# Attention layer on one core: query, key and value weights split in SBUF and turned by DMA instead of TensorE

## The reference, cut to what matters

```python
xn = layernorm(x)                                   # 2048 x 512
q  = (xn @ wq).reshape(b, s, 16, 192)               # per head 128 "nope" + 64 "rope" columns
kva = xn @ wkv_a                                    # 128 latent + 64 rope columns
ckv = rmsnorm(kva[..., :128]) * kv_norm_scale
kv = (ckv @ wkv_b).reshape(b, s, 16, 256)           # per head k_nope (128), v (128)
scores = (q_nope @ k_nope^T + rope(q_pe) @ rope(k_pe)^T) * 192 ** -0.5, causal
out = softmax(scores) @ v, heads side by side @ wo
x + out + (xn @ sum_r factors[r]) / sqrt(8) + bias
```

## Time and profile before

| | us |
|---|---|
| median of 3 runs | 1497.58 |
| profiled execution, first to last instruction (its span) | 1496.9 |
| PE busy | 1469.3 (98% of the span) |
| DVE busy | 1014.5 (68%) |
| ACT busy | 965.7 (65%) |
| POOL busy | 911.3 (61%) |
| DMA queue of SP | 74.2% of 16 engines |

### The profile page before, as it was taken

How to read it: one execution, slowest core, us unless ns; L and a number is a source line. 1 busy time by engine, 2 the same in 40 slices (tenths; PEclk the granted TensorE clock), 3 DMA queues, 4 the chain that set the end, 5 groups by cost and what they waited for, 6 DMA issues and landing times.

```text
span 1496.9 us, 25751 instructions
## 1 busy us (share of the span) xinstructions
PE 1469.3 (98%) x7908; PEld 755.5 (50%) x7908; DVE 1014.5 (68%) x2563; ACT 965.7 (65%) x2404; POOL 911.3 (61%) x919
## 2 busy tenths in 40 slices
PE   6999999999999999999999999999999999999998
PEld 5544555555555545445444444445545555555554
DVE  7877677877777766656556565556666666676777
ACT  7877767677876567566566666665546665654554
POOL 3688777776665456575465656566645655664553
PEclk9999999999999999999999999999999999999999
DMA  6599999988777597787577677886856677754564
GB/s 202 152 199 203 211 193 186 191 163 158 157 157 132 127 193 149 140 178 139 118 145 141 137 133 145 173 151 130 162 112 136 137 139 152 156 141 95 115 132 110
DMA packets 646615, 227.84 MB, mean 152 GB/s; under 512 B 599376, under 2 KB 612176, under 8 KB 646096
## 3 DMA queue, kind: packets, MB, share of 16 engines
q1 hardware_dynamic: 646480, 226.20, 74.2%
HBM read 65.67 MB, written 17.83 MB: 56 GB/s over the span
## 4 chain that ended last, share of the span: by engine, by line
PE 92%; POOL 2%; DVE 2%; ACT 2%; DMA 1%; issue 1%; SPq 0%; POOLq 0%; DVEq 0%; ACTq 0%
PE ps L426 18%; PE ps L428 18%; PE ps L427 18%; PE ps L577 7%; PE ps L582 7%; PE ps L583 7%; PE ps L578 7%; PE ps L579 7%; POOL st L1408 2%; ACT ex L812 1%; DMA acc<-x_in 0%; DVE stats L944 0%; PE ps L450 0%; DVE acc L1227 0%; DMA pT<-st 0%
## 5 line engine op out<-in xcount | busy, mean ns | idle before, releaser
L1408 POOL TENSOR_TENSOR st<-ex,st 128x512 f16<-128x512 f32 (+3 forms) x640 | 637.8, 1015 | 488.9 <-ACT st L822 478.8
L812 ACT ACTIVATE ex<-ps,nm,scales 128x512 f32<-128x512 f32 (+3 forms) x640 | 452.0, 709 | 456.3 <-DVE nm L1193 439.8
L1174 DVE TENSOR_REDUCE gm<-ps 128x1 f32<-128x512 f32 (+1 forms) x384 | 249.0, 669 | 170.0 <-PE ps L583 166.0
L822 ACT ACTIVATE st<-ex 128x512 f16<-128x512 f32 (+3 forms) x640 | 343.0, 562 | 6.1 <-ACT ex L812 0.4
L577 PE MATMUL ps<-kTh,q 128*128 128x512 f16 (+3 forms) x640 | 222.3, 347 | 4.5 <-ACT ex L812 2.1
L426 PE MATMUL ps<-pT,vH 128*128 128x512 f16 (+3 forms) x640 | 222.1, 347 | 2.9 <-DMA pT<-st 2.9
L582 PE MATMUL ps<-kRh,q 128*128 128x512 f16 (+3 forms) x640 | 222.2, 347 | 0.0
L583 PE MATMUL ps<-kRl,q 128*128 128x512 f16 (+3 forms) x640 | 222.1, 347 | 0.0
L579 PE MATMUL ps<-kTh,q 128*128 128x512 f16 (+3 forms) x640 | 222.1, 347 | 0.0
L578 PE MATMUL ps<-kTl,q 128*128 128x512 f16 (+3 forms) x640 | 222.1, 347 | 0.0
L427 PE MATMUL ps<-pT,vH 128*128 128x512 f16 (+3 forms) x640 | 222.1, 347 | 0.0
(11 more groups left out here) (202 smaller groups left out, 2144.3 us busy)
## 6 DMA issues: line engine op xcount, KB each, us to landing
wA<-w_abs SPq DMA_DIRECT2D x48, 256.0 KB, 2.9
wV<-w_vo SPq DMA_DIRECT2D x48, 256.0 KB, 2.9
pT<-st SPq DMA_TRANSPOSE x640, 3.2
fland<-factors_in SPq DMA_DIRECT2D x28, 256.0 KB, 3.1
wP<-w_pe SPq DMA_DIRECT2D x24, 256.0 KB, 3.0
wsq<-wq_in SPq DMA_DIRECT2D x16, 256.0 KB, 3.8
wso<-wo_in SPq DMA_DIRECT2D x16, 256.0 KB, 3.0
w_abs<-wA SPq DMA_DIRECT2D x16, 256.0 KB, 2.2
```

The lines of the kernel that those rows point to most:

```text
L812: e.activation(ex[:, n % NEX, 0:keys], s_bank(n)[:, 0:keys], ACT.Exp, bias=nm[:, (i * QT + r) % 4:(i * QT + r) % 4 + 1], scale=scales[:, p ...
L822: e.activation(stage(n, keys)[:, :, 0, :], ex[:, n % NEX, 0:keys].rearrange("p (t n) -> p t n", n=P), ACT.Copy).then_inc(z["a_pH"], 1)
L1174: e.tensor_reduce(m, b, AX_X, ALU.max).then_inc(z["v_max"], 1)
L1408: e.tensor_tensor(s[:, :, 1, :], ex[:, n % NEX, 0:keys].rearrange("p (t n) -> p t n", n=P), s[:, :, 0, :], ALU.subtract).then_inc(z["g_pL" ...
```

## The change

The split now comes before the turn. ScalarE reads fp32 weights in SBUF and writes the high parts into new tiles wtq and wtk (`wq_high`, `kv_high`), VectorE writes the low parts beside them (`wq_low`, `kv_low`), and SyncE issues one DMA_TRANSPOSE for the query part (`turn_wq`, 8 blocks of 128x128 fp16) and one for the key and value parts (`turn_kv`, 4 blocks; 2 where only one of them is due). TensorE's transposes and the PSUM banks that they took are gone; `w_abs` and `w_vo` wait for the DMAs. From unit 1 on, "wabs" moves from row 2 to the start of row 3; "wvo" stays in row 2. The high parts are in ScalarE's list at the end of row 0 (unit 0: row 1), the low parts in VectorE's at row 1 (unit 0: row 2), the turns in SyncE's list behind the row-1 transposes (unit 0: behind those of row 2).

```diff
@@ fills @@
-        out += [[("tq", 1), ("tkv", 1), ("sq1", 2)], [("wabs", 1), ("nrm", 2), ("wpe", 2)],
+        out += [[("sq1", 2)], [("wabs", 1), ("nrm", 2), ("wpe", 2), ("tq_hi", 2), ("tkv_hi", 2)],
                 [("tq", 2), ("tkv", 2), ("q", 1), ("wpe_low", 2)], [("wabs", 2)]][r]
...
+    if r == 3 and i and i + 2 < H:
+        out.insert(0, ("wabs", i + 2))
     if r == 0:
-        if i % 2 and i + 2 < H:
-            out.append(("tq", i + 2))
+        if i and i + 2 < H:
+            out.append(("tq_hi", i + 2))
+        if i and i + 2 <= H + 2:
+            out.append(("tkv_hi", i + 2))
...
     if r == 1:
         if i and i % 2 == 0 and i + 2 < H:
-            out += [("wpe", i + 2), ("tq", i + 2)]
+            out.append(("wpe", i + 2))
+        if i and i + 2 < H:
+            out.append(("tq", i + 2))
         if i and i + 2 <= H + 2:
             out.append(("tkv", i + 2))
...
     if r == 2:
         if 1 <= i <= H:
             out.append(("wvo", i - 1))
-        if i and i + 2 < H:
-            out.append(("wabs", i + 2))
@@ TensorE @@
             def w_abs(h):
-                e.wait_ge(z["v_tq"], h + 1)
-                e.wait_ge(z["v_tkv"], h + 1)
+                e.wait_ge(z["d_tq"], 16 * (h + 1))
+                e.wait_ge(z["d_tkv"], 16 * (h + 1))
...
             def w_vo(h):
                 e.wait_ge(z["v_wo"], h + 1)
-                e.wait_ge(z["v_tkv"], h + 4)
+                e.wait_ge(z["d_tkv"], 16 * (h + 4))
@@ ScalarE @@
+            def wq_high(h):
+                e.wait_ge(z[f"d_wq{h % 2}"], 16 * (h // 2 + 1))
+                e.wait_ge(z["v_w2"], h // 2 + 1)
+                if h:
+                    e.wait_ge(z["d_tq"], 16 * h)
+                e.activation(wtq[:, :, 0, :], wsq[:, h % 2, :, :], ACT.Identity, bias=eps[:, 2:3],
+                             scale=scales[:, h // 2, 0:1]).then_inc(z["a_tq"], 1)
@@ VectorE @@
+            def wq_low(h):
+                e.wait_ge(z["a_tq"], h + 1)
+                e.scalar_tensor_tensor(out=wtq[:, :, 1, :], in0=wsq[:, h % 2, :, :], scalar=scales[:, h // 2, 0:1],
+                                       in1=wtq[:, :, 0, :], op0=ALU.mult, op1=ALU.subtract).then_inc(z["v_tq"], 1)
@@ SyncE @@
+            def turn_kv(m):
+                e.wait_ge(z["v_tkv"], m + 1)
+                if m:
+                    e.wait_ge(z["p_wabs"], min(m, H))
+                if m > 3:
+                    e.wait_ge(z["p_wvo"], m - 3)
+                e.dma_start_transpose(wKV[:, kv_blocks(m), :, :].rearrange("p b a n -> p (b a) n"),
+                                      wtk[:, kv_blocks(m), :, :].rearrange("p b a n -> p (b a n)")).then_inc(
+                    z["d_tkv"], 16)
...
             store_chunk(0)
+            turn_wq(0)
+            turn_kv(0)
...
             store_pe(0)
+            turn_wq(1)
+            turn_kv(1)
...
                         for p in range(chunk(i) + 1):
                             transpose(i, r, p)
+                    if r == (1 if i else 2):
+                        if i + 2 < H:
+                            turn_wq(i + 2)
+                        if i + 2 <= H + 2:
+                            turn_kv(i + 2)
```

More of the change, by code:

```diff
@@ L203, in fills @@
     return out
-IN_BANKS = ("q", "pe", "tkv", "wvo", "tq", "wabs", "out", "ffn")
+IN_BANKS = ("q", "pe", "wvo", "wabs", "out", "ffn")
 SOON = {"nv": 0, "nf": 1, "out": 2, "tq": 3, "q": 4, "nrm": 5}
@@ L224, in bank_order @@
             pre.append(("nrm", 0))
-        if t == 11:
-            pre += [("tq", 0), ("tkv", 0)]
         if t == 12:
@@ L256, in build @@
         wa = sb("wa", [P, 2, KE, QH], F16)
-        wX = sb("wX", [P, 2, E], F16)
-        wKV = sb("wKV", [P, 2, 2 * P], F16)
+        wX = sb("wX", [P, KE, 2, P], F16)
+        wKV = sb("wKV", [P, 2, 2, P], F16)
+        wtq = sb("wtq", [P, KE, 2, P], F16)
+        wtk = sb("wtk", [P, 2, 2, P], F16)
         wsq = sb("wsq", [P, 2, KE, P], F32)
@@ L414, in pair, with kv_blocks, kv_parts @@
             return i % H // 2
-        def kv_cols(m):
-            return slice(0 if m < H else P, 2 * P if m >= 3 else P)
+        def kv_blocks(m):
+            return slice(0 if m < H else 1, 2 if m >= 3 else 1)
+        def kv_parts(m):
+            parts = []
+            if m < H:
+                parts.append((0, wsk[:, m % 4, :], scales[:, m // 2, 1:2]))
+            if m >= 3:
+                parts.append((1, wsv[:, m % 2, :], vsc[:, m - 3, 0:1]))
+            return parts
         block = ctx.enter_context(nc.Block())
@@ L478, in w_abs @@
                 b = free_bank(("wabs", h))
-                e.wait_ge(z["v_tq"], h + 1)
-                e.wait_ge(z["v_tkv"], h + 1)
+                e.wait_ge(z["d_tq"], 16 * (h + 1))
+                e.wait_ge(z["d_tkv"], 16 * (h + 1))
                 for k4 in range(KE):
                     cols = slice(k4 * P, (k4 + 1) * P)
-                    ins = three(b[:, cols], [wX[:, a, cols] for a in range(2)], [wKV[:, a, 0:P] for a in range(2)])
+                    ins = three(b[:, cols], [wX[:, k4, a, :] for a in range(2)], [wKV[:, 0, a, :] for a in range(2)])
                 ins.then_inc(z["p_wabs"], 1)
@@ L488, in w_vo @@
                 e.wait_ge(z["v_wo"], h + 1)
-                e.wait_ge(z["v_tkv"], h + 4)
-                three(b, [wKV[:, a, P:2 * P] for a in range(2)], [wV[:, h % 2, a, :] for a in range(2)]).then_inc(
+                e.wait_ge(z["d_tkv"], 16 * (h + 4))
+                three(b, [wKV[:, 1, a, :] for a in range(2)], [wV[:, h % 2, a, :] for a in range(2)]).then_inc(
                     z["p_wvo"], 1)
@@ L771, in w_pe, with kv_high @@
                              scale=scales[:, i // 2, 4:5]).then_inc(z["a_wpe"], 1)
+            def wq_high(h):
[5 more added lines that the diff above has]
+                             scale=scales[:, h // 2, 0:1]).then_inc(z["a_tq"], 1)
+            def kv_high(m):
+                if m < H:
+                    e.wait_ge(z["g_sk"], m // 2 + 1)
+                    e.wait_ge(z["v_w2"], m // 2 + 1)
+                if m >= 3:
+                    e.wait_ge(z["g_sv"], m - 2)
+                    e.wait_ge(z["v_vw"], m - 2)
+                if m:
+                    e.wait_ge(z["d_tkv"], 16 * m)
+                for part, w, size in kv_parts(m):
+                    ins = e.activation(wtk[:, part, 0, :], w, ACT.Identity, bias=eps[:, 2:3], scale=size)
+                ins.then_inc(z["a_tkv"], 1)
             def w_o(h):
@@ L1080, in kv_transpose, with kv_low @@
+            def kv_low(m):
+                e.wait_ge(z["a_tkv"], m + 1)
+                for part, w, size in kv_parts(m):
+                    ins = e.scalar_tensor_tensor(out=wtk[:, part, 1, :], in0=w, scalar=size, in1=wtk[:, part, 0, :],
+                                                 op0=ALU.mult, op1=ALU.subtract)
                 ins.then_inc(z["v_tkv"], 1)
@@ L1599, in transpose, with turn_wq @@
                     stage(n, keys).rearrange("p t a n -> p (t a n)")).then_inc(landed(n)[0], 16)
+            def turn_wq(h):
+                e.wait_ge(z["v_tq"], h + 1)
+                if h:
+                    e.wait_ge(z["p_wabs"], h)
+                e.dma_start_transpose(wX[:, :, :, :].rearrange("p k a n -> p (k a) n"),
+                                      wtq[:, :, :, :].rearrange("p k a n -> p (k a n)")).then_inc(z["d_tq"], 16)
+            def turn_kv(m):
+                e.wait_ge(z["v_tkv"], m + 1)
+                if m:
+                    e.wait_ge(z["p_wabs"], min(m, H))
[4 more added lines that the diff above has]
+                    z["d_tkv"], 16)
             load_x(0)
```

90 lines of the change are left out of this document (24 added, 66 removed).

## The result

The changed kernel takes **1575.36 us** (median of 4 runs, 1571.6 to 1576.65); the kernel before took 1497.66 beside it. The ratio is **1.051, 95% interval 1.050 to 1.053**. The forecast was 1557 with a range of 1538 to 1592: the direction and the mechanism held, and the time came out 18 us higher. In every run of both kernels the time lies 1.8 to 1.9 us above the span; the 0.7 us of the prediction came of setting the median of the runs beside the span of an execution that was itself about 1 us longer than the median.

A forecast was written before the change was run, and what follows sets the result against it. TensorE, busy 98% of the span, was taken as the bound: 1496.9 + 52 (W_vo) + 11.8 (W_abs(2)) - 8.8 (transposes) - 1.1 (idle) + 0.5 (preamble) + 5 (clock) = 1556.3, plus 0.7 for the median: 1557 us, range 1538 to 1592.

The forecast's parts named there:

- W_vo waits for a turn: Row 2 of units 1 to 16: W_vo waits for turn_kv, some 16 times, together 52 us (40 to 62).
- W_abs(2): Unit 0: it waits for turns behind row (0, 2)'s transposes; TensorE goes on 11.8 us later, idle 12.9.
- a wait in one unit does not shorten the next: W_vo's wait comes again in each unit, as the distance from scores to turn lies within the unit.
- sign of being wrong: The prediction would be wrong if, among other signs, W_vo waited under 2 us.
- Transposes: TensorE's 96 transposes go, 10.4 us; the 81 after W_abs(2) gain 8.8 us in full if nothing waits.
- TensorE's own list sets the pace: From unit 1 on: a matmul taken out is time won, a wait put in is time lost, one for one.
- Preamble: Head 0's turns, queued behind a 1 MB store, land at 44.6 to 46; 0.5 us, bounds -0.5 and 1.5.
- TensorE's clock: Clock falls at the new waits: 2 us for the 13 us gap, 3 for the 16 shorter; 0 to 2.6 each.
- Rival 1: The clock falls in every wait, 16 waits at 2.0 to 2.6 us each; about 1590 us, chance 0.15.
- Rival 2: SP or the DMA engines fall behind: share 0.91 to 0.97, turns landing 1.5 us later; 1581 us, chance 0.10.
- Rival 5: Nothing waits, SP issuing the turn before the row's transposes, so removed transposes are pure gain; 1487 us, chance 0.04.
- The busy time: TensorE's busy time falls by about 10 us if the clock holds; if it falls, busy time stays or grows.

The follow-up runs named there:

- e1: The changed kernel with W_vo of head i-1 one row later, in row (i, 3) behind W_abs; 1511.4 us, ratio 1.008.
- e4: The changed kernel with the turns issued ahead of row (i, 1)'s transposes in units 1 to 16, unit 0 left as it was; 1505.5 us, ratio 1.005.
- e8: e6 with unit 1's turns (head 3's blocks, first value block) also done by TensorE; 1497.9 us, ratio 0.9998.
- e10: e8 with W_vo(1) a row later and the reloads of heads 0 to 3's raw weights waiting for TensorE's transposes again; 1497.3 us, ratio 0.9992.
- e5: e4 with head 2's turns also ahead of row (0, 2)'s transposes and head 0's ahead of store_chunk(0); 1500.4 us, ratio 1.0013.
- e6: e4 with query and key blocks of heads 0 to 2 turned by TensorE as in the kernel before; 1500.4 us, ratio 1.0014.
- e2: The changed kernel with unused 512-column matmuls added ahead of the waits for turned blocks to keep TensorE busy; 1557.7 us, ratio 1.040.
- e9: The changed kernel with turn_kv issued ahead of turn_wq in units 1 to 16, both still behind the row's transposes; 1546.2 us, ratio 1.031.
- e3: The kernel before with the change's 16 + 19 DMA transposes added at the same places on SP, read by nobody; 1505.1 us, ratio 1.004.
- e7: e3 without the added transposes of heads 0 to 2, so only those of units 1 to 16 stay; 1500.9 us, ratio 1.0018.

## Why the prediction was right, and where it was 18 us off

- **W_vo waits for a turn: right.** 52 expected, 48.0 measured, in 15 places, unit 12 without one. Unit 6 came out at 15.5 us from scores to landing (15.7 foretold) and 3.53 us of wait (4.1). The odd units 3, 5, 7 and 13 waited 2.45 to 2.49 us (3.3 foretold), since there SP was 10.2 us behind the scores, not the 11.1 of the earlier trace rows; units 9 and 11, with SP 10.8 and 11.3 behind, waited 3.35 and 3.55. e1 and e4 show the mechanism. The price was read in units 5 and 6 alone, and that it fits units 1 to 3 is partly luck: there the kernel before has SP 20.6, 17.3 and 13.8 us behind, not 11 to 12, and it was the wait of W_abs(2) that had brought this down to 11.1, 11.8 and 10.2. The prediction's "a wait in one unit does not shorten the next" fails in these units (e8, e10). One wait, 1.46 us in unit 15, was under the 2 us that it had named as a sign of being wrong.
- **W_abs(2): right.** 12.9 us of idle time expected, 11.95 measured, and the 1.06 us of the earlier trace rows are gone. e5 shows that SP's order makes 7.5 of it.
- **Transposes: right in price, a little less in effect.** 0.65 us a unit is there in units 3, 5, 7 and 13 of e6. In the even ones from 4 to 10 0.28 go back to ScalarE's exponents, which the prediction counted at nothing ("TensorE's own list sets the pace"). Beyond that VectorE's and ScalarE's new work costs nothing to be seen.
- **Preamble: too low.** 0.5 expected, with 1.5 as the upper bound; the scores (0, 0) start at 57.00 instead of 54.48, 2.5 us. The turn that I had landing by 46 landed at 47.4: behind the 1 MB store `turn_wq(0)` and `turn_kv(0)` took 2.1 us each to issue where those of unit 6 took 1.2, and 6.9 and 4.9 from issue to landing. With them ahead of the store (e5) they take 1.4 and 1.2 us to issue and 5.3 and 4.2 to land, and W_abs(0) waits 0.48 us. So the store accounts for only part of the slow landing; what makes the rest is open. The two issues in the changed kernel:

```profile
40.34 2.14 SPq L1607 DMA_TRANSPOSE wX<-wtq  x1
42.53 2.09 SPq L1617 DMA_TRANSPOSE wKV<-wtk  x1
```

- **TensorE's clock: the term that was mis-sized.** 5 us expected, 22.7 measured. The step reads "I take 2 us for the 13 us gap and 3 for the 16 shorter ones together". The price of most falls was inside its bounds (1.7 us measured, 0 to 2.6 given; the two stretches of 6.8 us cost 2.7 and 2.9); the count was wrong: 11 of the 15 waits of W_vo had one. The long gap cost 2.3. With 22.7 in place of 5 and 2.5 in place of 0.5 the sum is 1576.7, and with 48.0 for 52 it is 1572.7, 2.7 below the measured time. About 1 us of that is the longer profiled execution named at the start, and 1.7 are what the ledger leaves over. Rival 1 named the mechanism and had it too strong: not every wait had a fall, a fall mostly cost 1.7 and not 2.0 to 2.6 us, and the measured time lies between its 1590 and the forecast's 1557. I gave it 0.15 because a gap of 1.06 us had done nothing, which says nothing of one three times as long. The sentence of the Trainium skill that I had set beside it (TensorE: Matmul & The Clock Gate, Part 1: The HAM clock gate), that an array left idle falls back to half speed, agrees with what e2 shows: with the array kept busy, no fall is left at W_abs(2) or at any W_vo. That it needs no long idle time is seen too, as waits of 2.09 and 2.12 us (e9) had a fall while others of up to 2.73 had none.
- **Rival 2** had its number right, a DMA share of 0.97 (e3), and its effect wrong: landing went from 3.2 to 3.3 us. **Rival 5** told what the cure is, the turn ahead of the row's transposes; e4 does just that from unit 1 on. It brings the time to 1505.5, not to 1487: unit 0 keeps its 11.9 us there, and where its turns are moved up too (e5), 4.4 of them stay.
- The busy time was to fall by 10 us or, if the clock falls, to grow: it grew by 13.7.

## What to carry to other kernels

Work moved from a full engine to a DMA costs the place of its issue in the queue plus its landing, not its duration: find the instruction that reads it, and put the issue ahead of the backlog or the reader behind it (70 or 64 of 78 us here). On an engine that is busy 98% of the time price each new wait of about 2 us or more with the clock as well, 1.7 us for most falls here. And read the queue's lag in the first units too, not in steady state alone: a backlog that the first units have even in the kernel before made the last wait walk from unit 1 to 2 to 3 as each was cured, and made that unit 8.9, 6.2 and 4.3 us longer.

## What the runs showed of the hardware that I had not expected

- In the changed kernel the granted clock fell to 0.5 at waits of 3.3 to 4.5 us in nine of nine cases, mostly for 3.4 us, which cost 1.7 us each; between 2.0 and 2.8 us some waits had a fall and some did not.
- Two waits of 3.1 us (e8, e10) had a fall too, and one of 2.5 us in e1 (W_abs(0)); the same wait of 2.4 us in the changed kernel had none. The shortest with a fall behind them were one of 1.97 us in the preamble of e5 and one of 1.45 us in e7, which follows another of 0.36 us; 1.75 us in e5 and 1.77 in e3 had none.
- 35 more DMA transposes raised the DMA engines' share from 0.92 to 0.97, and the median landing of pT went only from 3.2 to 3.3 us (e3). In the changed kernel the two behind a 1 MB store landed after 6.9 and 4.9 us in place of 3.3 and 2.3, and ahead of it (e5) still after 5.3 and 4.2.
